# Sentinel rows at the head of each region, and the second layer's inputs scaled by two engines

## The chip, the cores and the metric

The kernel runs on one core of a Trainium2 chip. The metric is the device time of one execution in microseconds; the median over several executions is compared. The engines are TensorE (PE), VectorE (DVE), ScalarE (ACT), GpSimd (POOL) and SyncE (SP), which here only issues transfers.

## The reference

The input `x` is 128 graphs of 128 nodes with 128 features, `adj` one 128x128 matrix per graph. Four stages follow each other, each added to the residual and each behind a layer norm without weights:

```python
x = x + gnn0(layernorm(x), adj)   # h = x W + b; u = adj * exp(e_i + f_j + a_b); (u / sum u) h
x = x + ffn0(layernorm(x))        # 30 times: h += 0.01 tanh(h); silu; layernorm; h W + b
x = x + gnn1(layernorm(x), adj)   # relu(x G_1 + (adj x) G_2 + bias)
x = x + ffn1(layernorm(x))        # per token: top 2 of 8 experts, gelu(x W1_e + b1_e) W2_e + b2_e
```

There are 16384 tokens. In the last stage each token's two experts form one of 28 pairs.

## The kernel before, in words

The graphs are worked on in 16 groups (`STREAMS`) of 8 tiles, a tile being 128 rows by 128 features. Every engine has its own program written out by hand, and semaphores (`wait_ge`, `then_inc`) set the order between the engines; within an engine instructions run in the order in which they are written. Work is skewed by lags: in slot k of a stage, each operation handles group k minus its lag.

**Iterations and tail.** The 30 iterations are a loop over slots, 16 per iteration. After the loop comes a tail of 16 slots (`iteration(STEPS, tail=True)`). In tail slot k TensorE turns a group for slots 0 to 12 (`flip`, L1084, PSUM ring buffer) once VectorE has freed that buffer (`x2_ready`), and multiplies the group turned in the slot before by the weights (`rows`, L1090 and L1094). Between the two ScalarE copies the turned tiles out of PSUM (L957). VectorE adds the product to the residual (L691), takes statistics (L661) and computes the variance (L665), for which it waits until GpSimd has finished the power of four groups before (`x2_pow`). GpSimd, after its last iteration, fills some constant tiles, and then does for each group: the power -1/2 of the variances (L485), the scaling of the 8 tiles of the residual (L550), and a copy of the token numbers (L552).

**Second graph layer** (`GNN1_SLOTS`, 23 slots). TensorE turns the scaled inputs of group k (L1084), ScalarE copies them out (L1021), TensorE multiplies them by the lower weights (`psQ`), ScalarE copies that to `values` (L1024), and TensorE mixes with the adjacency (`psM`, L1094). VectorE finishes the rows (L779), routes the tokens, counts them by pair (`find_slots`, L825 to L835), and so gets each token's slot: its row in the DRAM tensor `sorted_rows`, where each pair has a region of its own. GpSimd scatters each tile of 128 rows of 532 bytes there with one indirect DMA (L556), eight per group, and between the fourth and the fifth it computes the power for a later group (L578). In the last four groups (`s is None`) it waits before every four scatters until all its scatters before have landed.

**Tables, rows of no token.** When all slots are known, VectorE computes tables (L874 to L908): for each of 156 slabs of 128 rows, its first row in `sorted_rows` and its two experts. A region's last slab is not full, so behind the last token of each region 128 rows of no token are written by 29 copies of `pad_rows` (L384), 10 issued by SyncE, 19 by ScalarE, at addresses read from `pad_row`. Their token number lies outside the output, so the final scatter leaves them out.

**Experts.** SyncE loads per slab the rows (L427) and two experts' weights (L434). It begins with four weight loads, and then waits for all fills (`pads_in`) and all scatters (`scattered`) before the first rows. GpSimd computes a scale per row (L591), VectorE normalizes (L918), TensorE turns (L1246) and multiplies (L1256, L1265), ScalarE does gelu (L1044), VectorE adds up, and GpSimd stores the slab by an indirect DMA (L596) to the rows that the token numbers name.

Of the kernel before, what the change touches and what calls it, by code (L numbers as in the profile page):

```python
# [5 lines left out]
F32 = mybir.dt.float32  # L6
# [8 lines left out]
P = 128  # L15
# [3 lines left out]
def network(nc, x, adj, W_w, W_b, a_w, a_b, ln_w, ln_b, F_W, F_b, G_w, G_b,  # L19
# [25 lines left out]
    REGION = TOKENS + SLAB  # L45
# [15 lines left out]
    with ExitStack() as ctx:  # L61
# [29 lines left out]
        psT = [psum[:, j, 0:3 * P].rearrange("p (v j) -> p v j", v=3) for j in range(2)]  # L91
# [37 lines left out]
        pair_steps = sb("pair_steps", [P, 4, PAIRS])  # L129
        slab_j = sb("slab_j", [P, 2])  # L130
        frac = sb("frac", [P, P])
# [12 lines left out]
        pad_row = sb("pad_row", [P, PAIRS], I32)  # L144
        slab_ends = [sb(f"slab_ends{j}", [P, PAIRS]) for j in range(2)]
        past = sb("past", [P, 2, PAIRS])
        past_steps = sb("past_steps", [P, 2, 4, PAIRS])
        slab_is = sb("slab_is", [P, 2, 4])
        slab_has = sb("slab_has", [P, 2, 3])
        slab_row = sb("slab_row", [P, 2 * P], I32)  # L150
        slab_exp = sb("slab_exp", [P, 2 * P, 2], I32)
        pad = sb("pad", [P, ROW], I32)
# [49 lines left out]
        diag = over_resid(15, 1)[:, 0:6 * P].rearrange("p (h v j) -> p h v j", h=2, v=3)  # L202
# [12 lines left out]
        pad_rows = nc.dram_tensor("pad_rows", (SLAB, ROW), F32, kind="Internal").ap()  # L215
# [50 lines left out]
        x2_scaled = sem("x2_scaled")  # L266
        x2_flip = sem("x2_flip")
# [15 lines left out]
        ends_ready = sem("ends_ready")  # L283
# [15 lines left out]
        pad_out = sem("pad_out")  # L299
# [4 lines left out]
        scale_pow = sem("scale_pow")  # L304
        rows_normed = sem("rows_normed")
# [48 lines left out]
        PEELED = PEEL_EACH * (GNN0_SLOTS - PEEL_FROM)  # L354
        Q_LAG, MIX_LAG, X3_LAG, ROWS_LAG, ROUTE_LAG, RANK_LAG, PLACE_LAG = 1, 2, 3, 4, 5, 6, 7
# [18 lines left out]

        def by_queue(rows):
            return rows.rearrange("r c -> (r c)").rearrange("(q n) -> q n", q=16)

        def fill(queue, c):
            if c < PAIRS:
                at = queue.value_load(pad_row[0:1, c:c + 1], min_val=c * REGION, max_val=c * REGION + TOKENS)  # L380
                dst = sorted_rows[bass.ds(at, SLAB), :]
            else:
                dst = sorted_rows[PAIRS * REGION:PAIRS * REGION + SLAB, :]
            queue.dma_start(by_queue(dst), by_queue(pad_rows)).then_inc(pads_in, 16)  # L384

        SP_FILLS = 10

        @block.sync
        def _(sp):
# [50 lines left out]
            for c in range(SP_FILLS):  # L440
                fill(sp, c)
# [22 lines left out]
        def _(pool):  # L464
# [98 lines left out]
            for k in range(STREAMS + SCATTER_LAG):  # L563
                s, m = in_flight(k, 0, SCATTER_LAG)
                if m is not None:
# [3 lines left out]
                    if s is None:  # L569
                        pool.wait_ge(scattered, 16 * TILES * m)  # L570
# [743 lines left out]
```

## Time and profile before

| what | value |
| --- | --- |
| median of 3 runs | 2563.8 us (2562.12 to 2568.02) |
| profiled execution, its own time | 2566.49 us |
| its span | 2564.7 us |
| busy PE, PEld, DVE, ACT, POOL | 2378.7, 2320.6, 2081.9, 1811.9, 2027.5 us |
| granted TensorE clock, mean | 0.969 |

The time contains the span and what lies around it. Busy time is per engine; PE are matmuls, PEld weight loads that overlap them. A row of an engine in order of time gives the start, the duration, the line and tiles, how many instructions are merged, and in brackets the idle time before and what ended it. SPq is SyncE's queue of transfers.

### The profile page before, as it was taken

The numbers are of one execution on the slowest core, as the hardware profiler recorded it, in microseconds if no ns is written. First come the engines' busy times: TensorE is split into PE (matmuls) and PEld (weight loads), VectorE is DVE, ScalarE is ACT, GpSimd is POOL, SyncE is SP. The second block draws the span as 40 slices with busy tenths as digits, with TensorE's granted clock in tenths as the row PEclk, the third lists the DMA queues.
The fourth block names the chain that finished last, engine by engine and source line by source line (L and its number), as shares of the span: only waits on it lengthen the run. The fifth ranks groups of instructions, "written<-read, shape, count | busy, mean of one in ns | idle before, by whom it ended". The sixth has DMA issues, their size and how long they took to land.

```text
span 2564.7 us, 60894 instructions
## 1 busy us (share of the span) xinstructions
PE 2378.7 (93%) x19678; PEld 2320.6 (90%) x19935; DVE 2081.9 (81%) x5761; ACT 1811.9 (71%) x2185; POOL 2027.5 (79%) x1592
## 2 busy tenths in 40 slices
PE   6829999999999999999999999999862999999998
PEld 5829999999999999999999999989861999999998
DVE  5999999999999999999999999987572444444443
ACT  3779999999999999999999999833210334344333
POOL 4769999999999999999999999995764444444443
PEclk9969999999999999999999999999885999999999
DMA  9100000000000000000000000003223555555554
GB/s 261 69 1 1 0 0 0 0 0 0 0 0 0 0 0 0 0 0 0 0 0 0 0 0 0 0 18 110 75 73 109 212 216 212 211 214 216 212 212 148
DMA packets 121574, 164.56 MB, mean 64 GB/s; under 512 B 14982, under 2 KB 74018, under 8 KB 121360
## 3 DMA queue, kind: packets, MB, share of 16 engines
q1 hardware_dynamic: 111792, 145.12, 16.6%
q0 software_dynamic: 9088, 17.14, 2.0%
q10 hardware_dynamic: 608, 1.30, 0.2%
q8 instruction: 37, 0.61, 0.1%
q14 instruction: 49, 0.40, 0.0%
HBM read 40.40 MB, written 24.65 MB: 25 GB/s over the span
## 4 chain that ended last, share of the span: by engine, by line
DVE 58%; PE 31%; issue 7%; POOL 1%; DMA 1%; ACT 1%; SPq 1%; another core or an unknown queue 0%; DVEq 0%; POOLq 0%; ACTq 0%
DVE pair_stats L661 25%; DVE state L704 18%; PE psum L1265 11%; PE psum L1256 11%; DVE state L683 6%; PE psum L1094 5%; PE psum L1084 2%; DVE it_vars L665 2%; DVE x_stats L661 1%; POOL sorted_rows L556 1%; DVE resid L731 1%; PE psum L1213 1%; DMA sorted_rows<-state,slot 1%; PE psum L1246 1%; DVE state L700 1%
## 5 line engine op out<-in xcount | busy, mean ns | idle before, releaser
L1094 PEld LDWEIGHTS psum<-w_ffn,turned 128*128 128x128 f32 x7680 | 1010.1, 192 | 36.0
L1094 PE MATMUL psum<-w_ffn,turned 128*128 128x128 f32 x7680 | 1013.7, 275 | 12.8 <-issue 0.2
L512 POOL TENSOR_TENSOR it_rstd<-it_vars,minus_half 128x8 f32<-128x8 f32 x480 | 785.5, 1636 | 0.0
L515 POOL TENSOR_TENSOR state<-state,it_rstd 128x768 f32<-128x768 f32 x480 | 708.0, 1475 | 37.6
L661 DVE BATCH_NORM_STATS2 pair_stats<-state 128x6 f32<-128x256 f32 x1920 | 685.1, 418 | 0.0
L1084 PE MATMUL psum<-ident,state 128*128 128x128 f32 x4352 | 595.6, 281 | 59.1 <-DVE state L700 42.8
L704 DVE SCALAR_TENSOR_TENSOR state<-state,psum 128x1024 f32<-128x1024 f32 x464 | 560.8, 1209 | 1.8 <-ACT state L964 0.9
L1084 PEld LDWEIGHTS psum<-ident,state 128*128 128x128 f32 x4352 | 479.5, 143 | 78.0 <-issue 57.7
L957 ACT COPY turned<-psum 128x1024 f32<-128x1024 f32 x480 | 485.8, 1012 | 80.4 <-PE psum L1084 43.9
L967 ACT ACTIVATE state<-state 128x1024 f32<-128x1024 f32 x480 | 512.7, 1068 | 28.6 <-DVE state L700 9.1
L964 ACT ACTIVATE state<-psum 128x1024 f32<-128x1024 f32 x464 | 481.0, 1037 | 0.0
L1044 ACT ACTIVATE adjT<-psum 128x512 f32<-128x512 f32 x312 | 186.3, 597 | 283.3 <-PE psum L1256 262.9
L925 DVE TENSOR_TENSOR resid<-psum,adjT 128x128 f32<-128x128 f32 x312 | 91.0, 292 | 305.1 <-PE psum L1265 209.2
L1265 PE MATMUL psum<-resid,adjT 128*128 x2496 | 330.0, 275 | 2.0 <-DVE resid L925 2.0
L1256 PE MATMUL psum<-resid,adjT 128*128 128x128 f32 x2496 | 330.9, 276 | 0.0
L683 DVE TENSOR_SCALAR state<-state,it_rstd 128x128 f32<-128x128 f32 x960 | 318.5, 372 | 0.0
L1265 PEld LDWEIGHTS psum<-resid,adjT 128*128 128x128 f32 x2496 | 303.6, 192 | 2.6 <-issue 2.4
L1256 PEld LDWEIGHTS psum<-resid,adjT 128*128 128x128 f32 x2496 | 304.8, 193 | 0.0
L1090 PE MATMUL psum<-bias_mv,ones_bf 128*128 128x512 bf16 x736 | 279.7, 380 | 0.0
L596 POOL DMA_INDIRECT out_dram<-resid,adjT x156 | 161.1, 1033 | 129.0 <-DVE resid L930 96.7
L591 POOL TENSOR_TENSOR row_scale<-adjT,minus_half 128x1 f32<-128x1 f32 x156 | 89.3, 572 | 208.6 <-DMA adjT<-sorted_rows 205.5
L556 POOL DMA_INDIRECT sorted_rows<-state,slot x128 | 125.3, 979 | 81.7 <-issue 37.1
(190 smaller groups left out, 1725.2 us busy)
## 6 DMA issues: line engine op xcount, KB each, us to landing
adjT<-resid SPq DMA_DIRECT2D x312, 320.0 KB
adjT<-sorted_rows SPq DMA_DIRECT2D x156, 66.5 KB, 1.8
resid<-in_x_dram SPq DMA_DIRECT2D x16, 512.0 KB, 7.3
state<-in_adj_dram SPq DMA_DIRECT2D x16, 512.0 KB, 7.3
adjT_dram<-adjT SPq DMA_DIRECT2D x7, 512.0 KB, 3.7
adjT<-adjT_dram SPq DMA_DIRECT2D x7, 512.0 KB, 3.5
out_dram<-resid,adjT POOLq DMA_INDIRECT x156, 2.4
sorted_rows<-state,slot POOLq DMA_INDIRECT x128
```

Of the source, the lines that this page charges most:

```text
L512: nc.gpsimd.tensor_tensor(it_rstd[s % 8][:, :], it_vars[s % 4][:, :], minus_half[:, 0:TILES], ALU.pow).then_inc(it_pow, 1)
L515: nc.gpsimd.tensor_tensor(values[s][:, 0:POOL_TILES, :], values[s][:, 0:POOL_TILES, :], wide(it_rstd[s % 8][:, 0:POOL_TILES]), ALU.mult).t ...
L661: last = nc.vector.bn_stats(dst[:, i, :], src[:, 2 * i:2 * i + 2, :].rearrange("p t d -> p d t"))
L683: last = nc.vector.tensor_scalar(values[r][:, t, :], values[r][:, t, :], it_rstd[r % 8][:, t:t + 1], None, ALU.mult)
L704: nc.vector.scalar_tensor_tensor(values[k], values[k], 0.01, ring[k % 4], ALU.mult, ALU.add).then_inc(state_read, 1)
L957: nc.scalar.copy(turned[s % 4], ring[s % 4]).then_inc(it_turned, 1)
L964: nc.scalar.activation(values[k], ring[k % 4], ACT.Tanh).then_inc(tanh_done, 1)
L967: nc.scalar.activation(values[v], values[v], ACT.Silu).then_inc(silu_done, 1)
L1084: last = nc.tensor.transpose(dst[:, t, :], src[:, t, :], ident[:, :])
L1094: last = nc.tensor.matmul(dst[:, t, :], stationary(t), moving(t), start=bias is None and m == 0, stop=m == len(terms) - 1, skip_group_chec ...
L1256: last = nc.tensor.matmul(psH[o % 4][:, c, :], w1[:, c * P:(c + 1) * P], turned_T[o // 2 % 4], start=True, stop=True)
L1265: last = nc.tensor.matmul(psY[o % 2], hidden[o % 4][:, c, :], w2_all[:, bass.ds(e, 1), c, :].rearrange("p o d -> p (o d)"), start=c == 0, ...
```

## The change

It has two parts.

First, each region begins with 128 rows of no token instead of ending with them. They lie at places that are known in advance, so that one transfer on SyncE writes all 28 of them, with one more for the block behind the regions, before the second graph layer. The slots begin behind them (`region_0` has base SLAB). A region's last slab is moved back so that it ends with the last token; it then repeats rows of the slab before, or reaches into the rows of no token. New tables say how many rows are repeated (`slab_skip`), and an integer add on GpSimd per slab (`store_at`) puts the repeated rows' token numbers outside the output. The 29 fills, `pad_rows`, `pad_row` and GpSimd's waits for its own scatters in the last four groups are gone.

Second, GpSimd scales tiles 0 to 3 of each group's input of the second layer, and ScalarE tiles 4 to 7, with four activations placed in its program three slots behind (`X2_LAG`).

```diff
-    REGION = TOKENS + SLAB
+    REGION = SLAB + TOKENS
...
+        X2_LAG, X2_POOL = 3, 4
...
         def _(sp):
...
+            sp.wait_ge(pair_tables, 1)
+            regions = sorted_rows[0:PAIRS * REGION, :].rearrange("(c r) w -> r c w", c=PAIRS)
+            no_token = pad[:, :].bitcast(F32)
+            sp.dma_start(regions[0:SLAB], no_token.unsqueeze(1).to_broadcast([P, PAIRS, ROW])).then_inc(pads_in, 16)
+            sp.dma_start(sorted_rows[PAIRS * REGION:PAIRS * REGION + SLAB, :], no_token).then_inc(pads_in, 16)
+
             for j in range(AWAY):
...
-            sp.wait_ge(pair_tables, 1)
-            sp.dma_start(pad_rows, pad[:, :].bitcast(F32)).then_inc(pad_out, 16)
             sp.wait_ge(x3_ready, 5)
...
-            sp.wait_ge(pad_out, 16)
-            sp.wait_ge(ends_ready, 1)
-            for c in range(SP_FILLS):
-                fill(sp, c)
             sp.wait_ge(tables_ready, 1)
...
-            sp.wait_ge(pads_in, 16 * (PAIRS + 1))
+            sp.wait_ge(pads_in, 16 * 2)
...
         def _(pool):
...
+            nc.gpsimd.memset(pair_steps[:, 4, PAIRS - 1:PAIRS], float(FAR))
-            nc.gpsimd.iota(region_0[:, :], pattern=[[REGION, PAIRS]], base=0, channel_multiplier=0,
+            nc.gpsimd.iota(region_0[:, :], pattern=[[REGION, PAIRS]], base=SLAB, channel_multiplier=0,
...
             for s in range(STREAMS):
+                if s >= 4:
+                    pool.wait_ge(x2_scaled_a, s - 3)
                 pool.wait_ge(x2_var_ready, s + 1)
                 rsqrt(x_rstd[s % 4][:, :], x_var[s % 4][:, :], x2_pow, s)
-                nc.gpsimd.tensor_tensor(values[s], resid[s], wide(x_rstd[s % 4][:, :]), ALU.mult
-                                        ).then_inc(x2_scaled, 1)
                 nc.gpsimd.tensor_copy(state[s][:, :, TOKEN].bitcast(I32), ids[:, s * TILES:(s + 1) * TILES])
+                nc.gpsimd.tensor_tensor(values[s][:, 0:X2_POOL, :], resid[s][:, 0:X2_POOL, :],
+                                        wide(x_rstd[s % 4][:, 0:X2_POOL]), ALU.mult).then_inc(x2_scaled, 1)
...
                     pool.wait_ge(slots_ready, m + 1)
-                    if s is None:
-                        pool.wait_ge(scattered, 16 * TILES * m)
                     scatter(m, range(TILES // 2))
...
                 if m is not None:
-                    if s is None:
-
-                        pool.wait_ge(scattered, 16 * (TILES * m + TILES // 2))
                     scatter(m, range(TILES // 2, TILES))
...
                 pool.wait_ge(slab_in[n % EACH], 16 * (n // EACH + 1))
+                nc.gpsimd.tensor_tensor(store_at[n % EACH][:, :], rows_in[n % EACH][:, TOKEN:TOKEN + 1].bitcast(I32),
+                                        slab_skip[:, n:n + 1], ALU.add).then_inc(store_known, 1)
...
             def store(n):
+                pool.wait_ge(store_known, n + 1)
                 pool.wait_ge(y_ready, n + 1)
...
-                    out_offset=bass.IndirectOffsetOnAxis(ap=rows_in[n % EACH][:, TOKEN:TOKEN + 1].bitcast(U32), axis=0),
+                    out_offset=bass.IndirectOffsetOnAxis(ap=store_at[n % EACH][:, :].bitcast(U32), axis=0),
...
         def _(dve):
...
-            nc.vector.tensor_copy(pad_row[:, :], pair_end[:, :]).then_inc(ends_ready, 1)
+            nc.vector.tensor_scalar(part_of[:, :], slab_j[:, 0:1], 1.0 / P, None, ALU.mult)
+            nc.vector.tensor_tensor(pair_steps[:, 4, 0:PAIRS - 1], pair_end[:, 1:PAIRS], pair_end[:, 0:PAIRS - 1],
+                                    ALU.subtract)
...
-            table(nc.vector.tensor_scalar(slab_has[:, :, 0], slab_has[:, :, 0], float(SLAB), None, ALU.mult))
+            table(nc.vector.tensor_scalar(slab_from[:, :], slab_from[:, :], float(SLAB), float(SLAB), ALU.mult, ALU.add))
...
+            table(nc.vector.tensor_tensor(slab_last[:, :], slab_from[:, :], slab_last[:, :], ALU.min))
+            nc.vector.tensor_tensor(slab_has[:, :, 3], slab_from[:, :], slab_last[:, :], ALU.subtract)
+            nc.vector.tensor_scalar(slab_has[:, :, 0], slab_last[:, :], float(PAIRS * REGION), None, ALU.min)
...
+                nc.vector.tensor_scalar(slab_skip[:, h * P:(h + 1) * P], psT[h][:, 3, :], part_of[:, :], float(FAR),
+                                        ALU.is_gt, ALU.mult)
...
         def _(act):
...
-            iteration(STEPS, tail=True, slots=range(EVAC_LAG))
+            def scale_inputs(s):
+                act.wait_ge(x2_pow, s + 1)
+                for t in range(X2_POOL, TILES):
+                    last = nc.scalar.activation(values[s][:, t, :], resid[s][:, t, :], ACT.Copy,
+                                                scale=x_rstd[s % 4][:, t:t + 1])
+                last.then_inc(x2_scaled_a, 1)
+
+            for k in range(EVAC_LAG):
+                iteration(STEPS, tail=True, slots=range(k, k + 1))
+                if k >= X2_LAG:
+                    scale_inputs(k - X2_LAG)
...
                     nc.scalar.copy(turned[a % 3], psF).then_inc(x2_turned, 1)
+                if k < STREAMS - EVAC_LAG + X2_LAG:
+                    scale_inputs(k + EVAC_LAG - X2_LAG)
                 if b is not None:
...
-            act.wait_ge(pad_out, 16)
-            act.wait_ge(ends_ready, 1)
-            for c in range(SP_FILLS, PAIRS + 1):
-                fill(act, c)
...
         def _(pe):
...
                     pe.wait_ge(x2_scaled, a + 1)
+                    pe.wait_ge(x2_scaled_a, a + 1)
```

The tables `pair_steps`, `past_steps`, `slab_is` have 5 columns for 4, `slab_has`, `diag` and `psT` 4 for 3.

## Rows read from the trace of the kernel before

**Rows 1.** The page: its first line.

```profile
span 2564.7 us, 60894 instructions
```

**Rows 2.** Windows, expert stage: us; busy PE, PEld, DVE, ACT, POOL; clock; DMA share; GB/s.

```profile
2100.00:2200.00 100.00, 100.00 (x899) 100.00 (x898) 42.45 (x138) 39.72 (x81) 43.74 (x55) 1.00 0.59 212
```

**Rows 3.** In order of time, SyncE's queue from 1950 us.

```profile
1951.97 4.71 SPq L434 DMA_DIRECT2D adjT<-resid  x4
1974.81 2.60 SPq L427 DMA_DIRECT2D adjT<-sorted_rows  x3
```

**Rows 4.** In order of time, GpSimd's scatters.

```profile
1763.01 0.96 POOL L556 DMA_INDIRECT sorted_rows<-state,slot  x1 [0.30 <-issue]
...
1916.11 0.95 POOL L556 DMA_INDIRECT sorted_rows<-state,slot  x1 [2.15 <-DMA sorted_rows<-state,slot]
...
1971.72 0.96 POOL L556 DMA_INDIRECT sorted_rows<-state,slot  x1 [0.30 <-issue]
```

**Rows 5.** In order of time, VectorE: slots of groups 12 and 15, end of tables.

```profile
1914.76 0.17 DVE L835 CAST slot<-rank 128x8 int32<-128x8 f32 x1
...
1936.73 0.35 DVE L835 CAST slot<-rank 128x8 int32<-128x8 f32 x1
...
1946.21 0.42 DVE L908 TENSOR_SCALAR slab_exp<-psum 128x256 int32<-128x256 f32 x1
```

**Rows 6.** In order of time, GpSimd: group 0 of the second layer's inputs, group 1.

```profile
1672.37 1.63 POOL L485 TENSOR_TENSOR x_rstd<-x_var,minus_half 128x8 f32<-128x8 f32 x1
1674.07 1.90 POOL L550 TENSOR_TENSOR state<-resid,x_rstd 128x1024 f32<-128x1024 f32 x1
...
1676.07 1.64 POOL L485 TENSOR_TENSOR x_rstd<-x_var,minus_half 128x8 f32<-128x8 f32 x1
```

**Rows 7.** The page, DMA issues: KB each, us to landing.

```profile
state<-in_adj_dram SPq DMA_DIRECT2D x16, 512.0 KB, 7.3
```

**Rows 8.** Groups by line and shape, GpSimd, whole span: busy us, mean ns.

```profile
L515 POOL TENSOR_TENSOR state<-state,it_rstd 128x768 f32<-128x768 f32 x480 | 708.0, 1475 | 37.6
...
L506 POOL TENSOR_TENSOR shift<-shift,minus_one 128x8 f32<-128x8 f32 x16 | 3.2, 202 | 1.3
```

**Rows 9.** In order of time, TensorE: tail, start of the second layer, a later wait.

```profile
1670.27 1.06 PE L1084 MATMUL psum<-ident,state 128*128 128x128 f32 x8
...
1702.61 0.38 PE L1090 MATMUL psum<-bias_mv,ones_bf 128*128 128x512 bf16 x1
...
1704.82 1.04 PE L1084 MATMUL psum<-ident,state 128*128 128x128 f32 x8
1707.05 1.06 PE L1084 MATMUL psum<-ident,state 128*128 128x128 f32 x8 [1.19 <-ACT turned L1021]
1707.95 1.95 PE L1094 MATMUL psum<-w_mix,turned 128*128 128x128 f32 x16
...
1711.10 1.13 PE L1094 MATMUL psum<-w_mix,turned 128*128 128x128 f32 x8 [0.32 <-ACT state L1024]
...
1889.30 0.38 PE L1094 MATMUL psum<-w_mix,turned 128*128 128x128 f32 x2 [4.22 <-DVE state L779]
```

**Rows 10.** Waits from 1640 to 1990 us: total us, times, longest.

```profile
POOL sorted_rows L556 <- DVE slot L835: 25.2, 7, 9.5
...
PE psum L1084 <- DVE resid L691: 4.4, 8, 1.3
```

**Rows 11.** In order of time, ScalarE: first layer, tail slot 4, second layer.

```profile
104.25 3.19 ACT L972 ACTIVATE state<-resid,shift,x_rstd 128x128 f32<-128x128 f32 x8
...
1668.19 1.01 ACT L957 COPY turned<-psum 128x1024 f32<-128x1024 f32 x1 [2.17 <-PE psum L1084]
...
1705.89 1.01 ACT L1021 COPY turned<-psum 128x1024 f32<-128x1024 f32 x1 [4.29 <-PE psum L1084]
...
1709.94 1.02 ACT L1024 COPY state<-psum 128x1024 f32<-128x1024 f32 x1 [0.77 <-PE psum L1094]
```

**Rows 12.** Window in the second layer, columns as in rows 2.

```profile
1890.00:1895.00 5.00, 5.00 (x33) 4.85 (x32) 4.43 (x24) 0.00 (x0) 4.36 (x4) 0.68 0.18 55
```

More of the change, by code:

```diff
@@ L90, in network @@
         psW = psum[:, 7, :]
-        psT = [psum[:, j, 0:3 * P].rearrange("p (v j) -> p v j", v=3) for j in range(2)]
+        psT = [psum[:, j, :].rearrange("p (v j) -> p v j", v=4) for j in range(2)]
         resid_all = sb("resid", [P, STREAMS, TILES, D])
@@ L128, in network @@
         region_0 = sb("region_0", [P, PAIRS])
-        pair_steps = sb("pair_steps", [P, 4, PAIRS])
+        pair_steps = sb("pair_steps", [P, 5, PAIRS])
         slab_j = sb("slab_j", [P, 2])
+        part_of = sb("part_of", [P, 1])
         frac = sb("frac", [P, P])
@@ L143, in network @@
         pair_end = sb("pair_end", [P, PAIRS])
-        pad_row = sb("pad_row", [P, PAIRS], I32)
         slab_ends = [sb(f"slab_ends{j}", [P, PAIRS]) for j in range(2)]
         past = sb("past", [P, 2, PAIRS])
-        past_steps = sb("past_steps", [P, 2, 4, PAIRS])
-        slab_is = sb("slab_is", [P, 2, 4])
-        slab_has = sb("slab_has", [P, 2, 3])
+        past_steps = sb("past_steps", [P, 2, 5, PAIRS])
+        slab_is = sb("slab_is", [P, 2, 5])
+        slab_has = sb("slab_has", [P, 2, 4])
+        slab_from = sb("slab_from", [P, 2])
+        slab_last = sb("slab_last", [P, 2])
         slab_row = sb("slab_row", [P, 2 * P], I32)
         slab_exp = sb("slab_exp", [P, 2 * P, 2], I32)
+        slab_skip = sb("slab_skip", [P, 2 * P], I32)
+        store_at = [sb(f"store_at{j}", [P, 1], I32) for j in range(EACH)]
         pad = sb("pad", [P, ROW], I32)
@@ L266, in network @@
         x2_scaled = sem("x2_scaled")
+        x2_scaled_a = sem("x2_scaled_a")
         x2_flip = sem("x2_flip")
@@ L304, in network @@
         scale_pow = sem("scale_pow")
+        store_known = sem("store_known")
         rows_normed = sem("rows_normed")
@@ L372, in stages @@
                     yield base + j, j % STREAMS
[L375 to L386, printed above, removed]
         @block.sync
@@ L901, in _ @@
             for h in range(2):
-                last = nc.vector.tensor_tensor(diag[:, h], ident[:, :].unsqueeze(1).to_broadcast([P, 3, P]),
-                                               slab_has[:, h, :].unsqueeze(2).to_broadcast([P, 3, P]), ALU.mult)
+                last = nc.vector.tensor_tensor(diag[:, h], ident[:, :].unsqueeze(1).to_broadcast([P, 4, P]),
+                                               slab_has[:, h, :].unsqueeze(2).to_broadcast([P, 4, P]), ALU.mult)
             last.then_inc(diag_ready, 1)
```

13 lines of the change are left out of this document (5 added, 8 removed).

## The prediction

> **What bounds the kernel now.** I read the page first (span 2564.7 us [rows 1]), then windows of 50 and 5 us, then each engine in order of time from 1640 to 2010 us, where all of the change lies except one small GpSimd instruction per slab. Outside that stretch nothing is touched: the 30 iterations before it end the same way, and in the expert stage behind it TensorE is busy for all of 100 us in 100 [rows 2]. So the question is only when the expert stage starts. It starts when SyncE issues the first load of sorted rows at 1974.81 [rows 3], and that waits for the last scatter, whose issue ended at 1971.72 + 0.96 = 1972.68 [rows 4]. The chain of waits runs backwards through GpSimd's scatters to the slots of group 12 (ready at 1914.76 + 0.17 = 1914.93) [rows 5], from there through VectorE and TensorE in the second graph layer, and to the last iteration's tail (1657 to 1717 us), where GpSimd paces the work: it starts a group every 3.70 us, 1672.37 to 1676.07 [rows 6] (16 such periods), each made of a power (1.64), a 1024-wide product (1.90) and a small copy.
>
> **Part 1: the rows of no token.** Removed are 29 copies of 66.5 KB that SyncE (10) and ScalarE (19) issued after the last slot was known, the copy of `pad` to DRAM, and GpSimd's eight waits for its own scatters in the last four groups. What stands between the last scatters now: 32 of them take from 1916.11 to 1972.68, 56.6 us. Inside a run the pitch is 1.26 us (0.96 busy and 0.30 before it, at 1763.01 [rows 4]); 32 at 1.265 are 40.5 us. The slots come in time: group 15's at 1936.73 + 0.35 = 1937.1 [rows 5], before GpSimd reaches it. Starting at 1915.0 instead of 1916.1, the last issue would end at 1955.2 (the last pitch's pause left out), and with the 2.13 us that now lie between it and the first load (1974.81 - 1972.68) the loads would start at 1957.3. That is **-17.5 us**. Bounds for what the removed waits leave: 1.265 per scatter at best; at worst today's mean pace of 56.6 / 32 = 1.77, a gain of 0. I take the first, since the row of 1763.01 stands in a run without waits, less 0.5 for the four weight loads that now fall together with the last scatters: **-17.0**.
>
> Who is late next? The tables: VectorE ends them at 1946.21 + 0.42 = 1946.6 [rows 5]. New there are one instruction chained by a wait and some eight short ones (about 0.17 each, partly overlapped), wider ones (5 rows for 4, 4 diagonals for 3) and a TensorE product of 512 for 384 columns at the low clock: I add 2.3 us. SyncE then needs 4.71 us for the first four weight loads [rows 3]; from 1948.9 that ends near 1954.6, still 2.7 us before 1957.3. Covered, by little; without cover it would cost 2 us.
>
> The new transfer of 28 x 128 pieces of 532 B (1.9 MB) goes out at 1672, with no other transfer running, and SyncE's next load waits for the first mixed product (1717). Nearest row: 1024 pieces of 512 B (the 512 KB of adj per group) in 7.3 us [rows 7], so some 26 us for 3584. Nothing.
>
> **Part 2: half of the scaling to ScalarE.** GpSimd's period falls. Width 768 takes 1.475 [rows 8] and 1024 takes 1.90 [rows 6], so 512 about 1.05; the period is 3.70 - 0.85 = 2.85 to 2.9. Were GpSimd all that counts, 16 periods would give back 13 us. But TensorE needs 2.21 us for a product (1702.61 to 1704.82) and 0.90 for a turn (1707.05 to 1707.95) [rows 9], 3.11 per slot. So the most to be had is TensorE's idle time there: 4.4 us in eight waits for the residuals [rows 10], 1.19 and 0.32 at the layer's start [rows 9], about 6 us.
>
> Against this stands the order on ScalarE. In slot 3 of the tail it now runs `scale_inputs(0)`, which waits for `x2_pow` 1, and behind it in the queue stands the copy of slot 4, now at 1668.19 [rows 11]. The first power starts at 1672.37 [rows 6] (GpSimd is behind with the iterations and then sets constants, one more of them) and ends at 1674.07 with the new memset. Then come four scalings: eight of the same form (SBUF to SBUF, scale as a tensor) take 3.19 us [rows 11], a pitch of 0.39, so 1.55 for four; the copy starts at 1675.7, 7.5 us late. From such a copy's start to TensorE's next is 1.16 (1705.89 to 1707.05 [rows 9, 11]), so the product of slot 4 starts at 1676.9. Today it starts when slot 4's turn is over (1670.27 + 0.90 = 1671.2 [rows 9]). **TensorE stands idle for 5.7 us.** From there it is TensorE that paces: 3.11 per slot against 2.9 on GpSimd and 1.01 + 1.55 on ScalarE. Slot 13 ends at 1676.9 + 8 x 3.11 + 2 x 2.21 = 1706.2, where today it is 1704.82 [rows 9]: **+1.4**. So the gain of the split is more than eaten at the layer's start.
>
> Second, the clock. After TensorE had been idle for 4.22 us before 1889.30 [rows 9] its granted clock fell to 1.2 GHz, and 1890 to 1895 had a mean of 0.68 of 2.4 GHz [rows 12]: 3.2 us at the low level, half of it lost, 1.6 us. I take **+1.7**; below nothing if the clock holds (0), at most 3.3 if the low level lasts twice as long.
>
> Third, in the first slots of the next layer ScalarE still has groups 11 to 15. In slot 0 and 1 a scaling (1.55) stands before the copy of group 0's first product, today at 1709.94, and TensorE goes on 1.16 later, at 1711.10 [rows 9, 11]. The copy is pushed by 1.0 beyond the shift above: **+1.0**. Later slots have that slack. Together the second layer runs 4.1 us later, and the first scatter, which hangs on that pipeline, with it.
>
> **Part 3: the experts.** Each slab gets an integer add of 128x1 on GpSimd; the nearest row is 0.20 us [rows 8]. GpSimd is busy 43.74 of 100 us there [rows 2], so 156 of them are hidden under TensorE; once, at the start, it lies on the path: +0.2. The load addresses change, the number of slabs (156) and bytes do not.
>
> **Sum**: -17.0 + 1.4 + 1.7 + 1.0 + 0.2 = -12.7 us, if the shift of 4.1 reaches the scatters whole. The profiled execution took 2566.5 us (span 2564.7 and 1.8 around it), 2.7 above the median of the runs shown. 2566.5 - 12.7 = 2553.8; from the median of 2563.8 it is **2551.1 us**.
>
> **Rivals.** (a) *The split does what it is meant to*: ScalarE's wait costs nothing lasting, the layer starts up to 6 us earlier, and part 1 comes on top: 2563.8 - 17 - 6 = 2541. For it: TensorE's waits of [rows 10] are there. Against: the fixed order on ScalarE. (b) *The shift is absorbed*: GpSimd has 25.2 us of waits for slots in the second layer, 9.5 of them before the first scatter [rows 10], and if the others shrink the scatters start at the old time: 2547. Against: those waits are themselves waits for TensorE and VectorE. (c) *The scatters back up*: half of the removed waits come back as slow issues, 1.52 us per scatter: -8.5 + 4.3, 2560. For it: the last run falls together with VectorE's table work and the weight loads; against: the pitch of 1763.01 [rows 4] was kept while VectorE routed tokens. The Trainium skill, "SBUF — State Buffer", has a mechanism for such a stretch in its box on the "DVE blocks DMA" trap: while VectorE runs an instruction that uses both ports, GpSimd cannot write the descriptors of its DMAs. By that rule each short table instruction would hold up a scatter by its own length, and (c) would be likelier than I make it; no row read here shows a scatter held up that way. (d) *Slower*: the low clock does not end after ScalarE's hold-up but stays through the ten slots left in the tail, since each slot there leaves gaps. At half clock a slot costs up to 6.2 for 3.11 us, +3.1 each; from five slots on it outweighs the scatters, with all ten it is +31 - 12.7 = +18, 2582. Against: TensorE has no gap behind the hold-up, and the low stretch of [rows 12] ended after 3.2 us of work. (e) *The change does nothing there*, the waits were covered by something else such as instruction loading: 2564.
>
> **Chances.** Forecast 0.55, (a) 0.10, (b) 0.17, (c) 0.10, (d) 0.04, (e) 0.04. Changes within 0.2% (5.1 us) can hardly be told from none by this measurement. Faster by more: forecast, (a), (b) and a small part of the rest, 0.85; within: 0.10; slower: 0.05. The forecast's own bounds are -17.3 (nothing of the shift) and -6 (clock at its upper end, some of the backing up); the range reaches from 2545 to 2558, which holds it and (b), and leaves out (a), most of (c) and (d).
>
> **What would show it.** Right: in the tail, ScalarE's copy of slot 4 near 1675.7 behind four activations; an idle time of 5 to 6 us on TensorE before it; GpSimd's period 2.9; scatters in one run of 32 at 1.26; first load near 1961.5 (1957.3 + 4.1); tables done before. Wrong: the first mixed product at or before its old time (a); the first scatter late but group 12's not (b); scatters at 1.5 us or more (c); a clock row at 0.5 for most of 1677 to 1707 (d).

## The result and the profile after

The changed kernel takes 2551.72 us (median of 6 runs, 2549.30 to 2558.34), the kernel before, run beside it, 2563.92 (6 runs, 2561.05 to 2568.02). The ratio is **0.9955, 95% interval 0.9941 to 0.9969**; forecast were 2551.1 us and 2545 to 2558. One execution of the kernel before, among those beside the first four experiments, took 5842.03 us; the ratios leave it out. The profiled execution is the slowest of the six, 2558.34 us, so it lies 6.6 above its median, and the two traces differ by 8.2 us of span where the medians differ by 12.2. The page's first line [rows 1]:

```profile
span 2556.5 us, 61367 instructions
```

GpSimd at the start of the second layer's inputs, in order of time [rows 6]. The power starts 1.7 us later than before. The profiles give no sign that the change does this: in those of the changed kernel and of its variants below it starts between 1672.2 and 1674.1, in the other profiles between 1671.9 and 1673.9. The period is 1676.94 - 1674.09 = 2.85, as forecast (2.85 to 2.9).

```profile
1674.09 1.63 POOL L480 TENSOR_TENSOR x_rstd<-x_var,minus_half 128x8 f32<-128x8 f32 x1
1675.79 0.20 POOL L548 COPY state<-ids 128x8 int32<-128x8 int32 x1
1675.94 1.03 POOL L549 TENSOR_TENSOR state<-resid,x_rstd 128x512 f32<-128x512 f32 x1
1676.94 1.64 POOL L480 TENSOR_TENSOR x_rstd<-x_var,minus_half 128x8 f32<-128x8 f32 x1
```

ScalarE in the same stretch [rows 11]. It stands still for 8.05 us for the first power; the copy of tail slot 4 (L961) comes behind the four scalings (L1016), which take 1.28 together and let the copy start 1.19 after them.

```profile
1675.75 1.28 ACT L1016 ACTIVATE state<-resid,x_rstd 128x128 f32<-128x128 f32 x4 [8.05 <-POOL x_rstd L480]
1676.94 0.99 ACT L961 COPY turned<-psum 128x1024 f32<-128x1024 f32 x1
```

TensorE [rows 9]: idle for 4.95 us, then the first two half products at half speed (1.91 and 1.85 for eight matmuls, 1.05 at the full clock), then a turn of the second layer, the group's two first products, and later, in the routing, a wait that no other engine ends.

```profile
1671.96 1.06 PE L1095 MATMUL psum<-ident,state 128*128 128x128 f32 x8
1677.98 0.61 PE L1101 MATMUL psum<-bias_mv,ones_bf 128*128 128x512 bf16 x1 [4.95 <-ACT turned L961]
1678.38 1.91 PE L1105 MATMUL psum<-w_ffn,turned 128*128 128x128 f32 x8
...
1680.51 1.85 PE L1105 MATMUL psum<-w_ffn,turned 128*128 128x128 f32 x8
1682.20 1.04 PE L1095 MATMUL psum<-ident,state 128*128 128x128 f32 x8
...
1711.34 1.07 PE L1095 MATMUL psum<-ident,state 128*128 128x128 f32 x8 [1.19 <-ACT turned L1035]
1712.24 1.95 PE L1105 MATMUL psum<-w_mix,turned 128*128 128x128 f32 x16
...
1715.67 1.58 PE L1105 MATMUL psum<-w_mix,turned 128*128 128x128 f32 x12 [0.61 <-ACT state L1040]
...
1937.44 0.35 PE L1234 MATMUL psum<-hot,tri 128*128 128x224 bf16 x1 [5.90 <-issue]
```

The windows around the idle time: us; busy PE, PEld, DVE, ACT, POOL; granted clock; DMA share; GB/s. The mean is 0.53 up to 1680 and 0.78 behind it: the level is half, and full again before 1685.

```profile
1675.00:1680.00 5.00, 2.02 (x9) 1.93 (x10) 4.72 (x12) 3.56 (x10) 4.87 (x7) 0.53 1.13 214
1680.00:1685.00 5.00, 5.00 (x35) 4.77 (x34) 2.56 (x5) 3.78 (x9) 4.87 (x6) 0.78 1.24 175
```

GpSimd's scatters [rows 4]: the first of all, the first of the last 32, the two pauses over 0.31 us within these, the one among these that itself takes longer than 0.97 us, and the last one. No wait for a DMA is left; the 32 take 1963.94 - 1920.12 = 43.8 us (56.6 before, 40.5 forecast).

```profile
1759.38 1.22 POOL L554 DMA_INDIRECT sorted_rows<-state,slot  x1 [9.48 <-DVE slot L831]
...
1920.12 0.96 POOL L554 DMA_INDIRECT sorted_rows<-state,slot  x1 [1.76 <-DVE slot L831]
...
1940.73 0.96 POOL L554 DMA_INDIRECT sorted_rows<-state,slot  x1 [0.63 <-issue]
...
1944.85 0.97 POOL L554 DMA_INDIRECT sorted_rows<-state,slot  x1 [3.16 <-issue]
...
1953.71 1.37 POOL L554 DMA_INDIRECT sorted_rows<-state,slot  x1 [0.30 <-issue]
...
1962.98 0.96 POOL L554 DMA_INDIRECT sorted_rows<-state,slot  x1 [0.31 <-issue]
```

VectorE's slots of groups 12 and 15 and the end of the tables [rows 5], then SyncE's queue [rows 3]:

```profile
1919.15 0.17 DVE L831 CAST slot<-rank 128x8 int32<-128x8 f32 x1
...
1947.63 0.17 DVE L831 CAST slot<-rank 128x8 int32<-128x8 f32 x1
...
1959.37 0.42 DVE L912 TENSOR_SCALAR slab_exp<-psum 128x256 int32<-128x256 f32 x1
```

```profile
1960.71 5.21 SPq L433 DMA_DIRECT2D adjT<-resid  x4
1966.97 2.62 SPq L426 DMA_DIRECT2D adjT<-sorted_rows  x3
```

The expert stage starts at 1966.97, 7.84 us earlier than before. In parts: the first power 1.7 later; from there to group 12's slots 2.7 more (245.1 against 242.4); start of the last run of scatters -0.4; the run -12.8; from its end to the first load +0.9 (3.03 against 2.13); the rest of the program -0.4 (589.53 against 589.89). The sum is -8.3 (the spans differ by 8.2; the rest is rounding).

### The profile page after: what moved, and what is told of

Read it like the earlier page. It is cut to its first block, busy times and chain, and to the rows that moved or that the text cites. A ratio compares the mean times of both kernels' runs of the same rounds, so it can differ in the third digit from the quotient of the medians.

```text
span 2556.5 us, 61367 instructions
## 1 busy us (share of the span) xinstructions
PE 2398.7 (94%) x19934; PEld 2323.4 (91%) x19935; DVE 2073.2 (81%) x5767; ACT 1831.4 (72%) x2249; POOL 2041.4 (80%) x1749
## 4 chain that ended last, share of the span: by engine, by line
POOL 56%; PE 31%; DVE 6%; issue 4%; SPq 1%; ACT 1%; POOLq 1%; another core or an unknown queue 0%; DMA 0%; DVEq 0%
POOL it_rstd L507 30%; POOL state L510 26%; PE psum L1277 11%; PE psum L1268 11%; PE psum L1105 4%; PE psum L1095 2%; PE psum L1225 1%; DVE resid L727 1%; DVE x_stats L657 1%; PE psum L1258 1%; DVE pair_stats L657 1%; POOLq L506 1%; DVE state L736 1%; PE psum L1101 0%
## 5 line engine op out<-in xcount | busy, mean ns | idle before, releaser
L961 ACT COPY turned<-psum 128x1024 f32<-128x1024 f32 x480 | 485.9, 1012 | 60.9 <-PE psum L1095 24.6
L1101 PE MATMUL psum<-bias_mv,ones_bf 128*128 128x512 bf16 x992 | 377.3, 380 | 12.2 <-DVE state L775 7.3
L592 POOL DMA_INDIRECT out_dram<-resid,store_at x156 | 162.0, 1039 | 86.4 <-issue 48.8
L584 POOL TENSOR_TENSOR store_at<-adjT,slab_skip 128x1 int32<-128x1 int32 x156 | 28.9, 185 | 225.7 <-DMA adjT<-sorted_rows 216.6
L554 POOL DMA_INDIRECT sorted_rows<-state,slot x128 | 125.6, 981 | 68.2 <-issue 38.2
## 6 DMA issues: line engine op xcount, KB each, us to landing
adjT<-sorted_rows SPq DMA_DIRECT2D x156, 66.5 KB, 1.9
```

What stands on the lines that cost most here:

```text
L961: nc.scalar.copy(turned[s % 4], ring[s % 4]).then_inc(it_turned, 1)
L1101: nc.tensor.matmul(dst[:, 4 * bank:4 * bank + 4, :], ones_bf[:, :], bias_mv[bias][:, :, :], start=True, stop=False, skip_group_check=True)
```

## The experiments

The experiments ran on three chips, and the chips differ: the kernel before takes 2566.74 us beside the first four runs, 2552.17 beside the next four, 2550.18 beside the last three. So ratios to the kernel before on the same chip are compared.

**First four.** `rows_only` is part 1 alone: the changed kernel, with the scaling left to GpSimd.

```diff
-                nc.gpsimd.tensor_copy(state[s][:, :, TOKEN].bitcast(I32), ids[...])
-                nc.gpsimd.tensor_tensor(values[s][:, 0:X2_POOL, :], resid[s][:, 0:X2_POOL, :], ...)
+                nc.gpsimd.tensor_tensor(values[s], resid[s], wide(x_rstd[s % 4][:, :]), ALU.mult
+                                        ).then_inc(x2_scaled, 1)
...
-                    scale_inputs(k - X2_LAG)
```

> The rows of no token at the head of the regions, GpSimd's waits gone, but GpSimd scales all eight tiles as before. My theory: the gain is all in this part and the split costs 3 to 4 us, so about 15 to 17 us under the kernel before, 2547 to 2549, some 3 us under the changed kernel; TensorE not idle in the tail, first turn of the second layer 2.6 us earlier than in the changed kernel. Rival (the split helps or is neutral): 2552 or more. Where the tables and the weight loads are the last to come, part of the 3 us may stay hidden.

Measured: 2552.02 us (2550.68 to 2554.02), ratio 0.9945 (0.9931 to 0.9958), 14.7 less than the kernel before beside it. In its profile the tables and the weight loads come last: the loads end at 1955.00 + 6.11 = 1961.11, and the first rows are loaded at 1961.95, 4.48 us after the last scatter's end where it was 2.13.

`split_only` is part 2 alone, on the kernel before; `x_scaled`, free by then, counts ScalarE's scalings.

```diff
+                if s >= 4:
+                    pool.wait_ge(x_scaled, STREAMS + s - 3)
...
+                nc.gpsimd.tensor_tensor(values[s][:, 0:X2_POOL, :], resid[s][:, 0:X2_POOL, :], ...)
...
+                    scale_inputs(k - X2_LAG)
...
+                    pe.wait_ge(x_scaled, STREAMS + a + 1)
```

> The kernel before with only the scaling split over GpSimd and ScalarE. My theory: ScalarE's wait for the first power holds its copy of tail slot 4 back, TensorE idle for 5 us, its clock low for some us behind that, first turn of the second layer 2.6 to 3.1 us later; the time 3 to 4 us over the kernel before, 2567 to 2568. Rival (the split helps): 2558 to 2562. Rival (absorbed before the scatters): 2564.

Measured: 2569.10 us, ratio 1.0013 (1.0004 to 1.0022). **The split alone makes the kernel slower**, by 2.4 us in the medians; the interval reaches from 1.0 to 5.6 us. From the first power to the first scatter it takes 85.7 us where the kernel before takes 82.4 and `rows_only` 82.5; in the changed kernel it is 85.3.

`lag6` is the changed kernel with one constant changed, so that ScalarE scales a group three tail slots later.

```diff
-        X2_LAG, X2_POOL = 3, 4
+        X2_LAG, X2_POOL = 6, 4
```

> The changed kernel with X2_LAG 6 instead of 3, so that ScalarE scales group 0 only after its copy of tail slot 6, when the first power is done. My theory: no idle time of 5 us and no low clock in the tail, the first turn of the second layer 4 to 5 us earlier than in the kernel before and some 7 us earlier than in the changed kernel; the time 5 to 7 us under the changed kernel, about 2545, unless the tables and the weight loads come last, which move along with it. Rival (the order on ScalarE does not matter): the same as the changed kernel, 2551 to 2552.

Measured: 2547.42 us (2546.34 to 2552.30), ratio 0.9933 (0.9920 to 0.9947). ScalarE and TensorE of that trace in order of time, at the place where the changed kernel stands still: the scalings come at once behind the copies, and TensorE has no idle time behind 1664.66, where it waits 1.33 us for VectorE as the kernel before does (1.34 at 1663.90).

```profile
1675.34 1.01 ACT L961 COPY turned<-psum 128x1024 f32<-128x1024 f32 x1 [2.18 <-PE psum L1095]
1676.25 1.28 ACT L1016 ACTIVATE state<-resid,x_rstd 128x128 f32<-128x128 f32 x4
1678.46 1.01 ACT L961 COPY turned<-psum 128x1024 f32<-128x1024 f32 x1 [0.94 <-PE psum L1095]
```

```profile
1677.36 1.07 PE L1095 MATMUL psum<-ident,state 128*128 128x128 f32 x8
1678.48 1.05 PE L1105 MATMUL psum<-w_ffn,turned 128*128 128x128 f32 x8
...
1704.34 1.95 PE L1105 MATMUL psum<-w_mix,turned 128*128 128x128 f32 x16
```

The first power was at 1673.17 there, so the first product of the layer comes 31.2 us after it, against 38.2 in the changed kernel and 35.6 before; the first scatter comes 78.3 after it. Freed of the hold-up on ScalarE, the split is worth 4.2 us up to the first scatter (78.3 against 82.5 in `rows_only`). The changed kernel did not run beside it; by the ratios `lag6` is some 5.6 us under it (5 to 7 expected).

`rows_waits` is the changed kernel with GpSimd's eight waits for its own scatters put back.

```diff
+                    if s is None:
+                        pool.wait_ge(scattered, 16 * TILES * m)
                     scatter(m, range(TILES // 2))
...
+                    if s is None:
+                        pool.wait_ge(scattered, 16 * (TILES * m + TILES // 2))
                     scatter(m, range(TILES // 2, TILES))
```

> The changed kernel with GpSimd's eight waits for its own scatters in the last four groups put back. My theory: the waits are most of part 1, the last 32 scatters take eight times 6.4 us = 51 us where they now take 44 to 41; so 7 to 10 us slower than the changed kernel, about 2559 to 2562. Rival (the fills were what held the end, the waits cost nothing): 2552.

Measured: 2566.04 us, ratio 0.9998 (0.9988 to 1.0007). Slower than expected (2559 to 2562): with the waits back nothing is left of the gain over the kernel before. `rows_waits` still holds the split, though, and against `split_only` beside it, which holds the split too, it is 3.1 us less (the intervals just touch). The last 32 scatters take 55.1 us there and 57.3 in `split_only`; GpSimd's waits for groups 14 and 15 are shorter (2.29 and 2.21 us against 2.96 and 3.36), with no fills beside them. So while the waits are there, the fills seem to cost 2 to 3 us.

**Next four.** `changed_again` is the changed kernel unaltered, on another chip.

> The changed kernel once more, beside the others of this call, since chips differ by some us. 12 to 13 us under the kernel before. In its profile the slots of group 15 should again come 28 to 29 us after those of group 12 (28.5 in its first profile, 22.0 in the kernel before), if that delay belongs to scatters without waits and is no accident of one run.

Measured: 2538.45 us (5 runs), ratio 0.9947 (0.9933 to 0.9960), 13.7 less than the kernel before: the result again, on a faster chip. The second forecast failed: the slots of group 15 come 23.9 us after those of group 12, not 28 to 29. So that delay does not belong to scatters without waits alone.

`nowaits_fills` is the kernel before with nothing but the eight waits taken out. The 29 copies stay: they write from each pair's last slot on, the scatters below it.

```diff
-                    if s is None:
-                        pool.wait_ge(scattered, 16 * TILES * m)
...
-                    if s is None:
-
-                        pool.wait_ge(scattered, 16 * (TILES * m + TILES // 2))
```

> The kernel before with GpSimd's eight waits for its own scatters taken away and nothing else; the 29 fills stay. My theory: the waits are what part 1 gained, so the last 32 scatters take 44 to 46 us for 56.6 and the kernel is 10 to 13 us faster, 2551 to 2554 where the kernel before takes 2564; the fills, which SyncE and ScalarE issue from the tables' start on, keep SyncE from the weight loads and may hold the rows' first load by 1 to 3 us. Rival (the fills slow the scatters as soon as those are not paced, since both use the same engines): a gain of 0 to 5 us, 2559 to 2564.

Measured: 2536.36 us (2535.59 to 2537.16), ratio 0.9939 (0.9925 to 0.9953), 15.8 less than the kernel before (10 to 13 expected) and 2.1 less than the changed kernel beside it. **Two deleted waits in the source give the whole gain.** The 2.1 us beyond the change are about what the split costs, which this kernel does not have. The last 32 scatters take 44.6 us, and the first load follows their end by 2.12: the fills hold up neither.

`lag4` is the changed kernel with `X2_LAG, X2_POOL = 4, 4`.

> The changed kernel with X2_LAG 4. If the hold-up on ScalarE is the cause, its size goes with the slot that is held: with 3 the product of tail slot 4 starts 5.7 us late, with 4 that of slot 5 some 2.6 us (its copy is now at 1671.4 and would be at 1675.7), with 6 none. From the power of group 0 to the first scatter it took 85.3 us with 3, 82.4 in the kernel before, 78.3 with 6; with 4 it should be 80 to 82. Time 2 to 4 us under the changed kernel. Rival (what matters is the extra load on ScalarE in the second layer): 85 us and the changed kernel's time.

Measured: 2533.10 us, ratio 0.9927 (0.9911 to 0.9942), 5.35 less than the changed kernel (2 to 4 expected). First product 33.1 us after the first power (changed kernel here 38.4), first scatter 80.2 after it (85.5). ScalarE still waits 4.86 us for the first power there, but TensorE is idle for 1.76 only, and the first products behind that keep the full speed (1.05 for eight):

```profile
1676.18 0.39 PE L1101 MATMUL psum<-bias_mv,ones_bf 128*128 128x512 bf16 x1 [1.76 <-ACT turned L961]
1676.41 1.05 PE L1105 MATMUL psum<-w_ffn,turned 128*128 128x128 f32 x8
```

`waits_12_13` is the changed kernel with the waits back in groups 12 and 13 alone.

```diff
+                    if m in (12, 13):
+                        pool.wait_ge(scattered, 16 * TILES * m)
...
+                    if m in (12, 13):
+                        pool.wait_ge(scattered, 16 * (TILES * m + TILES // 2))
```

> The changed kernel with the waits put back in groups 12 and 13 only. Theory A: unpaced scatters hold up VectorE and TensorE in the last slots of the routing (they wait there for nothing that the profile shows), so with the waits back the slots of group 15 come 22 to 24 us after those of group 12, as in all runs with waits, where they took 28.5; the scatters themselves take 4 to 6 us more, so the time is 0 to 4 us over the changed kernel. Rival B (that delay comes from something else in the changed kernel, such as its larger code): still 28 us, and the time 4 to 6 us over the changed kernel.

Measured: 2546.29 us (10 runs), ratio 0.9976 (0.9967 to 0.9985), 7.8 more than the changed kernel beside it, 1.96 us for each of four waits. That is above both forecasts (0 to 4, and 4 to 6). Between theory A and rival B it decides nothing: the slots of group 15 come 23.9 us after those of group 12 here, and 23.9 also in `changed_again`, without waits. Of its last 32 scatters, in order of time, those with a pause over 0.31 us:

```profile
1905.00 0.95 POOL L554 DMA_INDIRECT sorted_rows<-state,slot  x1 [2.15 <-DMA sorted_rows<-state,slot]
...
1912.06 0.96 POOL L554 DMA_INDIRECT sorted_rows<-state,slot  x1 [1.61 <-DMA sorted_rows<-state,slot]
...
1920.17 0.96 POOL L554 DMA_INDIRECT sorted_rows<-state,slot  x1 [2.72 <-DMA sorted_rows<-state,slot]
...
1926.83 0.95 POOL L554 DMA_INDIRECT sorted_rows<-state,slot  x1 [1.64 <-DMA sorted_rows<-state,slot]
...
1936.59 0.96 POOL L554 DMA_INDIRECT sorted_rows<-state,slot  x1 [3.76 <-issue]
```

The four pauses for landings hold 8.12 us; less the usual 0.30 each, 6.9. Nearly all of the rest lies in the scatters themselves: six of the 32 take 1.06 to 1.40 us for the usual 0.96, 1.0 us more in all than the two such ones in `changed_again` (1.39 and 1.17). Such a scatter is explained below, under the rivals.

**Last three.** On this chip the kernel before takes 2550.18 us. `lag6_again` is `lag6` once more.

> The changed kernel with X2_LAG 6, as in the first call, now on the chip of this call. Theory (ScalarE's queue order costs the layer's start, and nothing else of the split costs): ratio to the kernel before 0.992 to 0.9935, first mixed product 31.2 us after the first power, no idle time of TensorE before the tail's products. Rival (the 5 us of the first call were a difference of that chip's stalled executions): ratio 0.9945 to 0.9955, as the changed kernel.

Measured: 2530.99 us (2530.34 to 2532.29), ratio 0.9925 (0.9912 to 0.9939), the fastest full version of the study together with `lag4` (0.9927) and `fills_lag6` (0.9926), which follows. The first product of the layer comes 31.2 us after the first power, as expected.

`fills_lag6` is the kernel before without the waits, with the split and a lag of 6: the copies of the rows of no token instead of the rows at the heads.

```diff
-        X2_LAG, X2_POOL = 3, 4
+        X2_LAG, X2_POOL = 6, 4
```

(against `split_only`, with the deletion of `nowaits_fills` beside it)

> The kernel before with GpSimd's eight waits taken out and the split with X2_LAG 6, its 29 copies of the rows of no token kept. Theory (all of part 1's gain is the removed waits; placing the rows at the heads of the regions gives nothing itself): within 2 us of lag6_again. Rival 1 (the copies share the DMA queues with the last scatters and delay their landing): 3 to 6 us slower than lag6_again, last scatter's end to the first load 4 us or more instead of 2.3. Rival 2 (the longer tables of the new placement cost at the end): 1 to 3 us faster than lag6_again.

Measured: 2531.86 us (2530.55 to 2533.69), ratio 0.9926 (0.9913 to 0.9940): the same as `lag6_again`. Its last scatter's end to its first load is 2.12 us, 2.32 in `lag6_again`. Once the waits are gone, where the rows of no token lie gives nothing and costs nothing that these runs can tell (0.9 us).

`no_row_power` is `lag6` with a copy in place of the power in GpSimd's 16 groups of the second layer. The normalisation of the logits is left out, and so the two weights per token differ; the choice of experts and the slots do not.

```diff
-                    nc.gpsimd.tensor_tensor(row_rstd[c][:, :], row_vars[c][:, :], minus_half[:, :], ALU.pow
-                                            ).then_inc(x3_pow, 1)
+                    nc.gpsimd.tensor_copy(row_rstd[c][:, :], row_vars[c][:, :]).then_inc(x3_pow, 1)
```

> As lag6_again, but GpSimd copies row_vars to row_rstd (about 0.2 us) where it takes the power (1.67 us) in the 16 groups of the second layer: the normalisation of the routing logits and so the two weights of each token are left out; the choice of experts, the slots and the number of slabs stay. Theory for an execution in which TensorE does not stall in the routing (profile of the second call: one chain on GpSimd from the first scatter to the last, 128 x 1.265 + 12 x 1.87 + one stall of 3.7 = 188 us, measured 187.5): twelve powers come out of the chain, 12 x 1.47 = 17.6 us less than lag6_again, last scatter 170 us after the first. Theory for an execution with TensorE's stalls as in the first call (204.6 us, GpSimd waits for slots): at most 4 us less. Rival (the scatters are not the bound even without stalls; VectorE's 9.8 us per group is): 0 to 8 us less.

Measured: 2521.52 us, ratio 0.9886 (0.9871 to 0.9901), 9.5 less than `lag6_again`: between the theory (17.6) and the rival (0 to 8). The last scatter ends 179.0 us after the first began, 187.4 in `lag6_again`. Its scatters show why not more: GpSimd, with 1.47 us less per group, now catches up with VectorE and waits for slots, 11.2 us at three places.

```profile
1858.04 0.96 POOL L554 DMA_INDIRECT sorted_rows<-state,slot  x1 [3.84 <-DVE slot L830]
...
1871.92 0.95 POOL L554 DMA_INDIRECT sorted_rows<-state,slot  x1 [4.00 <-DVE slot L830]
...
1885.15 0.95 POOL L554 DMA_INDIRECT sorted_rows<-state,slot  x1 [3.36 <-DVE slot L830]
```

So on this chip GpSimd is the bound from the first scatter to the last, and VectorE is close behind it: of 17.6 us taken out of GpSimd's chain, 8.4 come through to the last scatter.

## Why the prediction was right, point by point

**The waits.** Forecast for part 1: -17.0 for the scatters, +0.2 for the experts. `rows_only` gave -14.7. The step was right in kind, and the runs show that the waits are all of it or nearly so: back in, 0.9998; taken out alone, 0.9939. What the eight waits do to the last run is plain in `rows_waits` (55.1 us) and the changed kernel (43.8). The size was off. I priced the run at 32 x 1.265 = 40.5, and it took 3.3 more. Nearly all of that is a stall of 3.16 us, "issue", that no other engine ends; less the usual pause it is 2.9. The pause of 0.63 and the scatter of 1.37 add 0.3 and 0.4, and the pause before the first scatter (0.3) is not in the 43.8. The kernel before had the stall too (3.70 us) within its 56.6, so it was there to be read, and I booked it with the waits.

**Tables and weight loads.** "Covered, by little", by 2.7 us. The sum there is short by 1.0: 1948.9 + 4.71 is 1953.6, not 1954.6 (the 0.92 us that lie between the tables' end and the first weight load in the profile after were not named). In the profile after the cover is gone: the tables end at 1959.79, the weight loads at 1960.71 + 5.21 = 1965.92, and the first load follows the last scatter's end by 3.03 instead of 2.13, +0.9. The cause is the slots of group 15, which come 28.5 us after those of group 12 where it was 22.0; I had taken the old 22. In `rows_only` it is 28.7 and the step costs 2.35 us (4.48 for 2.13), about the 2 named for the case without cover. Why these slots come late stays open. On the chips where the kernel before takes 2564 to 2567 us, the three profiles without waits have 28.5 to 28.7 and the three with waits 22.0 to 23.0; on the faster ones all have 21.8 to 24.0. In the profile after, VectorE stands still for 4.80 us before 1944.23, just ahead of these slots, where the kernel before has 1.92. On the faster chips the question does not arise: in `changed_again` the tables end at 1926.2 and the last scatter at 1946.1.

**ScalarE's order.** Forecast: TensorE idle for 5.7 us before the product of slot 4; it was 4.95, with the product at 1677.98. Relative to the first power it was put at 1676.9 - 1672.37 = 4.5 and came at 3.9. Of the 0.6 between them 0.4 are the four scalings: 1.55 was taken from a form with scale and bias as tensors (3.19 for 8 [rows 11]); those of the tail have a scale alone and let the next copy start after 1.19. Then TensorE sets the pace (3.09 per slot without a wait; 3.11 forecast).

**The clock.** Forecast +1.7. Two half products at half speed and two bias matmuls take 1682.20 - 1677.98 = 4.22 us where the same four take 2.21 at full speed [rows 9]: +2.0. Together the first product of the layer comes 2.6 us later relative to the first power than before; forecast 3.1.

**The start of the second layer.** Forecast +1.0 for group 0's mixed product; it was 3.43 after the first product instead of 3.15, +0.3: scalings of 1.19 left room. The whole shift up to the first scatter is 2.9 us (3.3 in `split_only`), forecast 4.1.

**The sum.** -12.7 forecast, -12.2 measured, and by ratios 0.9945 for part 1 and 1.0013 for part 2 make 0.9958, measured 0.9955. Part 1 was taken some 2 us too large and the cost of part 2 some 1 to 2 too large; the errors cancel. That the time came within 1 us is luck; the mechanisms are not. Of the signs named, the first load near 1961.5 did not come true: it was at 1966.97. The late first power is 1.7 of that; 3.8 remain, which the run (3.3) and the gap behind it (0.9) more than hold.

**The rivals.** (a) *The split helps*: not as written, but `lag6` shows that it would with ScalarE's order mended: 2547.42 us against 2552.02 for `rows_only` beside it, 4.6 less (3.1 by the ratios, whose intervals overlap). `lag4` and `nowaits_fills`, which do not overlap, bear it out: 2533.10 against 2536.36 on one chip, 3.3 less, with the split and without it (and with the rows at the heads and without). (b) *The shift is absorbed*: no; `lag4` and the changed kernel, side by side, differ by 5.3 us up to the first scatter and by 5.35 in the time. (c) *The scatters back up*: not by half of the removed waits, but a little. The mean of the last 32 is 43.8 / 32 = 1.37 us, for 1.265 in my sum and 1.52 in (c), and most of the surplus is the one stall. The other pauses stay at 0.30 to 0.31 with one of 0.63, while VectorE works on slots and tables (10.85 us busy of the 20 from 1940 on):

```profile
1940.00:1960.00 20.00, 4.30 (x5) 1.18 (x4) 10.85 (x47) 0.00 (x0) 12.86 (x14) 0.53 0.14 45
```

But the hold-up that (c) names does exist; it shows in the duration of a scatter and not in the pause before it. The scatter of 1953.71 takes 1.37 us for the usual 0.96, and it starts while this instruction pair of VectorE runs:

```profile
1952.95 1.29 DVE L903 TENSOR_TENSOR resid<-ident,slab_has 128x512 f32<-128x512 f32 x2
```

The clearest case is one of VectorE's SCALAR_TENSOR_TENSOR instructions (L840, 0.69 us). In `changed_again`, VectorE first, then GpSimd:

```profile
1911.98 0.69 DVE L840 SCALAR_TENSOR_TENSOR resid<-resid 128x512 f32<-128x512 f32 x1
```

```profile
1912.11 1.39 POOL L554 DMA_INDIRECT sorted_rows<-state,slot  x1 [0.30 <-issue]
```

In the 13 profiles 37 scatters start in the first 0.5 us of such an instruction, and all 37 take longer, 1.04 to 1.45 us: the later they start in it, the less. The 62 that start in the 0.96 us before it take 0.95 to 0.97. So a scatter that meets a running instruction of this kind is held for the rest of it, and one that was there first is not. The profile of the kernel before has such a scatter (at 1899.13, 1.30 us), which I had not read. By the Trainium skill, "SBUF — State Buffer", the "DVE blocks DMA" trap, instructions of VectorE that use both ports would hold up the scatters; that is not every short instruction of the tables, as I wrote. The traces agree as to the hold-up; which of VectorE's instructions use both ports, no row tells. Its price is small, 0.4 us in the last 32 scatters of the profile after and 0.7 in those of `changed_again`. (d) *The clock stays low*: no, it is back before 1685. (e) *Nothing*: no.

## What to carry to other kernels

Before a wait is taken out together with a rearrangement, try the wait alone: here eight waits of about 2 us each were the whole gain, and the new placement of 28 x 128 rows, with longer tables, was worth nothing once they were gone. When work is given to an engine with a fixed order, look for the first instruction in its queue that will wait for the work's input, and write it so late that the input is there: three slots of lag turned a cost of 2.4 us into a gain. And a sum that fits is not yet a sum whose terms fit; two runs, each with one part alone, tell that.

## What the runs showed of the hardware

**A stall at a fixed place of GpSimd's program.** In every trace of the study, those of before and after among them, the 15th scatter from the last has a pause of 3.15 to 4.15 us in front of it, "issue", with nothing awaited. In the profile after it is the row of 1944.85, fourteen scatters ahead of that of 1962.98. In `changed_again` it is this one, with the last scatter 17.7 us behind it:

```profile
1927.50 0.97 POOL L554 DMA_INDIRECT sorted_rows<-state,slot  x1 [3.66 <-issue]
...
1945.18 0.96 POOL L554 DMA_INDIRECT sorted_rows<-state,slot  x1 [0.30 <-issue]
```

It falls together with different work of VectorE each time (there with the last of the tables, which end at 1926.2, in the profile after 15 us ahead of their end), so it belongs to the place in GpSimd's program, or to the count of its scatters (it stands before the 114th), and not to that work. The loading of instructions would be a guess at the cause, and the traces give it no support: in 12 of the 13 profiles no transfer of an instruction queue runs in that pause (in `no_row_power` one does). No run moved the place; the cause stays open.

**One program, two paces on different chips.** From the first scatter to group 12's slots the changed kernel takes 159.8 us in its first profile and 132.1 in `changed_again`. Windows of the first (columns as above):

```profile
1760.00:1800.00 40.00, 37.10 (x303) 36.04 (x301) 30.13 (x123) 10.52 (x17) 31.48 (x31) 0.91 0.43 139
1800.00:1840.00 40.00, 36.23 (x265) 34.81 (x265) 25.40 (x103) 10.58 (x16) 28.48 (x28) 0.83 0.28 95
```

and of `changed_again`:

```profile
1760.00:1800.00 40.00, 40.00 (x373) 39.70 (x372) 35.85 (x146) 13.71 (x21) 32.18 (x31) 1.00 0.43 141
1800.00:1840.00 40.00, 39.02 (x357) 37.99 (x355) 33.61 (x135) 12.81 (x20) 32.14 (x31) 1.00 0.26 97
```

In the slower one TensorE's routing products come one by one with nothing to wait for, and the half clock follows (2.63 us for 13 of them, 1.85 for 16 otherwise):

```profile
1775.49 0.26 PE L1225 MATMUL psum<-wr_c,turned 128*128 128x8 f32 x1 [0.44 <-issue]
...
1777.58 2.63 PE L1225 MATMUL psum<-wr_c,turned 128*128 128x8 f32 x13 [1.12 <-issue]
```

The profiles before and after and those of the first four runs have this pace (156.4 to 161.0 us for that stretch), those of the last seven the other (132.0 to 133.7). In the second GpSimd paces everything from the first scatter on: 128 x 1.265 + 12 powers at 1.87 + one stall of 3.66 make 188.0 us, and 187.5 were measured. Although the bound differs, the ratio of the change is the same within its interval (0.9955 and 0.9947). What makes TensorE stall on the one chip and not on the other stays open.

**Many small pieces.** The store of 28 x 128 pieces of 532 B landed in 12.8 us, half of the 26 that I had scaled from the 512 KB loads of `adj` [rows 7]; beside it ran only the 66.5 KB for the block behind the regions. From the page of that stretch, DMA issues: KB, us to landing.

```profile
sorted_rows<-pad SPq DMA_DIRECT2D x1, 1862.0 KB, 12.8
```
